# Attention's results stored by token, and the memory stage's first batch and weights loaded inside attention's last groups

## What is computed

```python
# 4 batches of 1024 tokens, 128 features, 16 heads of 8
q, k, v = heads(x @ w_attn.T + b_attn), ..., heads(x)
y_ar = softmax(causal(q @ k.T * scale)) @ v                 # attention
e    = v[1:] - y_ar[:-1]
qa, ka = -leaky_relu(-q[1:] * scale, 0.02), sigmoid(k2 * scale * 0.02)
y_ma = tril(qa @ ka.T) @ e                                  # memory, no softmax
out  = (y_ar + shift(y_ma)) @ w_proj.T + 2 * b_proj
```

## Time and profile before

| | us |
|---|---|
| median of 3 runs | 1926.33 |
| lowest and highest | 1923.79 to 1932.21 |
| profiled execution, its own time | 1940.25 |
| its span in the trace | 1938.2 |
| attention's last store issued | 626.4 |
| first DMA of memory | 628.6 |
| first DMA of ffn1 | 818.8 |
| PE busy share of the span | 72% |

### The profile page before, as it was taken

One profiled execution on the slowest core, in us unless ns is written; L12 is line 12 of the kernel. 1 busy time (PEld: TensorE's weight loads), 2 busy tenths in 40 slices (PEclk: granted clock), 3 DMA queues, 4 the chain that ended last, 5 costly groups with the idle time before them and its releaser, 6 DMA issues. The chain is left out here.

```text
span 1938.2 us, 29318 instructions
## 1 busy us (share of the span) xinstructions
PE 1394.9 (72%) x8975; PEld 721.5 (37%) x8976; DVE 1283.7 (66%) x2982; ACT 833.6 (43%) x1181; POOL 863.3 (45%) x761
## 2 busy tenths in 40 slices
PE   4459999999998488767598557586686545481992
PEld 1113333333332366644497222131131101351992
DVE  4567888888983144476233259999999998571333
ACT  3305666666666011122254267557466332120551
POOL 3401111121122333367366316876868665473662
PEclk9657999999999587878799778788797666796996
DMA  4721111111100765153232367785957763534335
GB/s 136 233 78 40 44 61 43 54 52 42 61 9 10 110 122 99 40 160 108 59 94 78 104 168 185 195 211 146 233 147 188 191 163 76 161 94 115 88 93 147
DMA packets 232076, 214.96 MB, mean 111 GB/s; under 512 B 66079, under 2 KB 201218, under 8 KB 229634
## 3 DMA queue, kind: packets, MB, share of 16 engines
q1 hardware_dynamic: 209934, 184.90, 37.6%
q0 software_dynamic: 9216, 19.02, 3.0%
q10 hardware_dynamic: 12800, 9.46, 1.6%
HBM read 149.46 MB, written 63.37 MB: 110 GB/s over the span
## 5 line engine op out<-in xcount | busy, mean ns | idle before, releaser
L772 ACT ACTIVATE attn_prob<-attn_ps_cols 128x1024 f32<-128x1024 f32 (+1 forms) x320 | 290.5, 940 | 231.1 <-PE attn_ps_cols L648 229.8
L2298 POOL TENSOR_TENSOR ssm_hc<-ssm_h,ssm_cb 128x1024 f32<-128x1024 f32 x128 | 301.4, 2356 | 169.8 <-DVE ssm_h L2281 122.3
L2281 DVE TENSOR_TENSOR_SCAN ssm_h<-ssm_decay,ssm_ps_u 128x1024 f32<-128x1024 f32 x128 | 292.6, 2286 | 17.2 <-DVE ssm_ps_u L2276 0.5
L798 POOL TENSOR_SCALAR_AFFINE_SELECT attn_prob<-attn_prob 128x512 f32<-128x512 f32 x128 | 81.2, 635 | 428.2 <-ACT attn_prob L772 428.2
L680 DVE CUSTOM_DVE_ANT_0 attn_ps_rows<-attn_ps_rows,const_mask_rows 128x384 f32<-128x384 f32 (+3 forms) x512 | 235.4, 521 | 42.6 <-PE attn_ps_rows L615 42.5
L615 PE MATMUL attn_ps_rows<-attn_ks,attn_qs 72*128 72x512 bf16 (+3 forms) x768 | 228.3, 351 | 42.3 <-DMA attn_qs<-parts_dram 29.1
L2232 PE MATMUL ssm_ps_u<-ssm_stack,ssm_spread 96*128 96x512 bf16 x256 | 100.3, 484 | 175.7 <-DVE ssm_h L2281 170.3
L2269 ACT ACTIVATE ssm_decay<-ssm_wide,ssm_aneg 128x1024 f32<-128x1024 f32 x128 | 146.0, 1146 | 179.0 <-DVE ssm_h L2281 120.6
L648 PE MATMUL attn_ps_cols<-attn_qs,attn_ks 75*128 75x512 bf16 (+3 forms) x768 | 194.4, 333 | 4.9 <-DMA attn_qs<-attn_nrows 4.1
L667 PE MATMUL attn_ps_o<-attn_prob,attn_vw 128*32 128x512 f32 (+3 forms) x1536 | 166.6, 506 | 0.3 <-POOL attn_prob L798 0.3
L685 DVE TENSOR_REDUCE attn_nm<-attn_ps_rows 128x1 f32<-128x512 f32 x256 | 157.7, 680 | 7.8 <-PE attn_ps_rows L615 7.8
(11 more groups left out here) (321 smaller groups left out, 2471.1 us busy)
## 6 DMA issues: line engine op xcount, KB each, us to landing
ssm_wide<-delta_dram SPq DMA_DIRECT2D x128, 512.0 KB, 6.4
attn_ks<-parts_dram SPq DMA_DIRECT2D x48, 192.0 KB
attn_qs<-parts_dram SPq DMA_DIRECT2D x48, 192.0 KB
parts_dram<-proj_parts SPq DMA_DIRECT2D x8, 768.0 KB, 3.8
ffn1e_x<-ex_dram SPq DMA_DIRECT2D x40, 130.0 KB, 2.3
ffn2e_x<-ex_dram SPq DMA_DIRECT2D x40, 130.0 KB, 2.2
split_dram<-ssm_parts SPq DMA_DIRECT2D x6, 768.0 KB, 4.4
ssm_stack<-split_dram SPq DMA_DIRECT2D x18, 256.0 KB, 4.3
```

The costliest lines, as they stand in the source:

```text
L772: nc.scalar.activation(prob[u % RING][:, heads[0]:heads[-1] + 1, 0:w], ps_cols[s % 2][:].rearrange("p b (x q) -> p (b x) q", x=len(heads) ...
L2281: nc.vector.tensor_tensor_scan(h[t % H_RING][:], decay[t % DECAY_RING][:], ps_u[t % 2][:], 0.0, ALU.mult, ALU.add).then_inc(scan_done, 1)
L2298: nc.gpsimd.tensor_tensor(hc[:, t % HC_RING, :], h[t % H_RING][:], cb[b % 2][:], ALU.mult).then_inc(hc_done, 1)
```

## The change

A class `Early` holds the tiles of even batches of the memory stage (rows, `kaT`, `qaT`, `yt`, `vs`, `x`, and the weights) and their semaphores. It is opened ahead of attention and given to both stages, so these tiles are there while attention runs. SP issues the loads of the weights and batch 0's rows after attention's group 12, and those of batch 0's `kaT`, `yt`, `vs`, `qaT` and `x` after group 13, behind a wait for the stores of batch 0's results. The memory stage's SP starts with batch 1. `yar` is laid out by token, 4096 by 128, and `yt` is one load a batch, in pieces of 128 numbers.

```diff
+class Early:
+    def load_rows(self, sp, dram):
+        feature = [dram["fT"][q].rearrange("(g d r) (b t) -> b r d g t", g=GPB, d=HD, b=B) for q in range(2)]
+        for r in range(RTILES):
+            sp.dma_start(self.kr[32 * r:32 * r + HD], feature[1][0, r]).then_inc(self.r_loaded, 16)
+            sp.dma_start(self.qr[32 * r:32 * r + HD], feature[0][0, r]).then_inc(self.r_loaded, 16)
+    def load_weights(self, sp, a):
+        sp.dma_start(self.wrow[:], a["w_proj"]).then_inc(self.w_loaded, 16)
+        sp.dma_start(self.brow[:], a["b_proj"].rearrange("(o n) -> o n", o=1).broadcast_to([P, P])).then_inc(self.w_loaded, 16)
+    def load_tokens(self, sp, dram, a):
+        sp.dma_start(self.kaT[:], dram["fT"][1, :, 0:T]).then_inc(self.ka_loaded, 16)
+        sp.dma_start(self.yt[:], dram["yar"][0:T, :].rearrange("(j p) d -> p j d", p=P)).then_inc(self.y_loaded, 16)
+        sp.dma_start(self.vs[:], dram["xn"][1:T + 1, :].rearrange("(j p) d -> p j d", p=P)).then_inc(self.v_loaded, 16)
+        sp.dma_start(self.qaT[:], dram["fT"][0, :, 0:T]).then_inc(self.qa_loaded, 16)
+        sp.dma_start(self.x[:], a["x"][0:T, :].rearrange("(j p) d -> p j d", p=P)).then_inc(self.x_loaded, 16)
...
 # attention
-        yar = dram["yar"].rearrange("g (c j p) n -> g c p j n", c=2, p=P)
+        yar = dram["yar"].rearrange("(b c j p) (g n) -> b g c p j n", b=B, c=2, p=P, g=GPB)
...
+                    if g == GROUPS - 4:
+                        early.load_weights(sp, a)
+                        early.load_rows(sp, dram)
+                    if g == GROUPS - 3:
+                        for ch in range(2):
+                            sp.wait_ge(y_stored[ch], GPB * 16)
+                        early.load_tokens(sp, dram, a)
...
 # memory
-            for g in range(GPB):
-                sp.dma_start(yt[k][:, :, g * GH * HD:(g + 1) * GH * HD], yar[i, g]).then_inc(y_loaded[k], 16)
+            sp.dma_start(yt[k][:], dram["yar"][i * T:(i + 1) * T, :].rearrange("(j p) d -> p j d", p=P)).then_inc(y_loaded[k], 16)
...
-                sp.dma_start(wrow[:], a["w_proj"]).then_inc(w_loaded, 16)
-                sp.dma_start(brow[:], a["b_proj"].rearrange("(o n) -> o n", o=1).broadcast_to([P, P])).then_inc(w_loaded, 16)
-                for i in range(B):
+                for i in range(1, B):
                     load_batch(sp, i)
```

More of the change, by code:

```diff
@@ L549, in bank_free, with __init__, attention @@
     return nth(g, same[-1] if same else -1)
-def attention(nc, dram, c):
+RTILES = 4
+class Early:
+    def __init__(self, nc, ctx):
+        self.m = m = Mem(nc, ctx, "early")
+        self.wrow, self.brow = m.sb("wrow", [P, P]), m.sb("brow", [P, P])
+        self.qr, self.kr = m.sb("qr", [P, GH, T]), m.sb("kr", [P, GH, T])
+        self.kaT, self.qaT = m.sb("kaT", [P, T]), m.sb("qaT", [P, T])
+        self.yt, self.vs, self.x = (m.sb(n, [P, BLK, D]) for n in ("yt", "vs", "x"))
+        self.w_loaded = m.sem("w_ld")
+        self.r_loaded, self.y_loaded, self.v_loaded, self.ka_loaded, self.qa_loaded, self.x_loaded = (
+            m.sem(n) for n in ("r_ld", "y_ld", "v_ld", "ka_ld", "qa_ld", "x_ld"))
+    def load_rows(self, sp, dram):
[12 more added lines that the diff above has]
+        sp.dma_start(self.x[:], a["x"][0:T, :].rearrange("(j p) d -> p j d", p=P)).then_inc(self.x_loaded, 16)
+def attention(nc, dram, c, early, a):
     with ExitStack() as ctx:
@@ L602, in store_y @@
             sp.sem_inc(passed, 1)
-            sp.dma_start(yar[at, ch], y[ch][:].rearrange("p j h d -> p j (h d)")).then_inc(y_stored[ch], 16)
+            sp.dma_start(yar[at // GPB, at % GPB, ch], y[ch][:].rearrange("p j h d -> p j (h d)")).then_inc(y_stored[ch], 16)
         def row_tile(k, n, loads, bank, free):
@@ L882 @@
 HALF = BLK // 2
-RTILES = 4
 AM_RING = 2
@@ L886, with memory @@
 HALVES = B * 2
-def memory(nc, dram, c, a):
+def memory(nc, dram, c, early, a):
     with ExitStack() as ctx:
         m = Mem(nc, ctx, "mem")
[L894 to L899, removed]
+        wrow, brow = early.wrow, early.brow
+        wT, bias2 = m.sb("wT", [P, P]), m.sb("bias2", [P, P])
+        qr, kr = [early.qr, m.sb("qr1", [P, GH, T])], [early.kr, m.sb("kr1", [P, GH, T])]
+        kaT, qaT = [early.kaT, m.sb("kaT1", [P, T])], [early.qaT, m.sb("qaT1", [P, T])]
+        yt, vs = [early.yt, m.sb("yt1", [P, BLK, D])], [early.vs, m.sb("vs1", [P, BLK, D])]
+        e = [m.sb(f"e{k}", [P, BLK, D]) for k in range(2)]
         ew = [m.sb(f"ew{k}", [P, BLK, HEADS, 32]) for k in range(2)]
         ka = [m.sb(f"ka{k}", [P, HALF, P]) for k in range(3)]
-        x, xb = ([m.sb(f"{n}{k}", [P, BLK, D]) for k in range(2)] for n in ("x", "xb"))
+        x = [early.x, m.sb("x1_in", [P, BLK, D])]
+        xb = [m.sb(f"xb{k}", [P, BLK, D]) for k in range(2)]
         x1 = [m.sb(f"x1{k}", [P, HALF, D]) for k in range(2)]
@@ L911, in memory @@
         ps_s = m.ps("ps_s", [P, UNIT])
-        w_loaded, w_turned, w_ready, bias_ready = (m.sem(n) for n in ("w_ld", "w_turned", "w_ready", "bias_ready"))
-        r_loaded, y_loaded, v_loaded, ka_loaded, qa_loaded, x_loaded = (m.pair(n) for n in ("r_ld", "y_ld", "v_ld", "ka_ld", "qa_ld", "x_ld"))
+        w_loaded = early.w_loaded
+        w_turned, w_ready, bias_ready = (m.sem(n) for n in ("w_turned", "w_ready", "bias_ready"))
+        r_loaded, y_loaded, v_loaded = [early.r_loaded, m.sem("r_ld")], [early.y_loaded, m.sem("y_ld")], [early.v_loaded, m.sem("v_ld")]
+        ka_loaded, qa_loaded, x_loaded = [early.ka_loaded, m.sem("ka_ld")], [early.qa_loaded, m.sem("qa_ld")], [early.x_loaded, m.sem("x_ld")]
         x1_stored = m.pair("x1_st")
@@ L921, in memory @@
         feature = [dram["fT"][q].rearrange("(g d r) (b t) -> b r d g t", g=GPB, d=HD, b=B) for q in range(2)]
-        yar = dram["yar"].rearrange("(b g) (j p) n -> b g p j n", b=B, p=P)
         def load_batch(sp, i):
@@ L966, in outputs @@
             if b == 0:
-                nc.tensor.wait_ge(y_loaded[k], (i // 2 + 1) * GPB * 16)
+                nc.tensor.wait_ge(y_loaded[k], (i // 2 + 1) * 16)
                 nc.tensor.wait_ge(qa_loaded[k], (i // 2 + 1) * 16)
@@ L1023, in make_e @@
             dve.wait_ge(v_loaded[k], n * 16 + 16)
-            dve.wait_ge(y_loaded[k], (n + 1) * GPB * 16)
+            dve.wait_ge(y_loaded[k], (n + 1) * 16)
             if i >= 2:
@@ L1182, in memory @@
         m.leave()
+        early.m.leave()
 EXPERTS, HIDDEN, TOP = 8, 256, 2
@@ L2618, in build @@
             "fT": scratch("fT_dram", (2, P, N)), "parts": scratch("parts_dram", (2 * PARTS, B, P, T), BF16),
-            "yar": scratch("yar_dram", (16, T, 32)), "x1": scratch("x1_dram", (N, D)),
+            "yar": scratch("yar_dram", (N, D)), "x1": scratch("x1_dram", (N, D)),
             "delta": scratch("delta_dram", (B, INNER, T)),
@@ L2628, in build @@
         project(nc, dram, c, {"x": rows, "w_attn": w_attn, "b_attn": b_attn, "w_k2": w_k2, "b_k2": b_k2})
-        attention(nc, dram, c)
-        memory(nc, dram, c, {"x": rows, "w_proj": w_proj, "b_proj": b_proj})
+        with ExitStack() as held:
+            early, rest = Early(nc, held), {"x": rows, "w_proj": w_proj, "b_proj": b_proj}
+            attention(nc, dram, c, early, rest)
+            memory(nc, dram, c, early, rest)
         ffn(nc, dram, c, experts, "ffn1", dram["x1"], None)
```

## The result

| | before | changed |
|---|---|---|
| median, us | 1929.27 (4 runs) | 1900.46 (4 runs) |
| lowest to highest | 1923.79 to 1936.92 | 1898.71 to 1908.86 |
| ratio | | 0.9842, 95% interval 0.9809 to 0.9875 |
| profiled execution | 1940.25 | 1898.71 |
| its memory stage | 190.2 | 158.1 |

The median fell by 28.8 us, against a forecast of 30.3. The forecast time, 1896.0 us, had been taken from the earlier median of 1926.33 (three runs); a fourth run moved that to 1929.27, and the measured 1900.46 is 4.5 us above the forecast and inside its range of 1874 to 1906. The length of the memory stage is taken here and in all experiments from POOL's first instruction of the stage to its first of ffn1. These two rows give it for the changed kernel, 781.90 - 623.76; before, they stand at 628.62 and 818.80.

What follows compares the result with a forecast made beforehand. PE was taken as the bound once it has its data, with loads costing late start, waits and clock. Savings 21.0 + 3.6 + 3.0 + 2.7 = 30.3 us off 1926.3 gave 1896.0 us, range 1874 to 1906.

Steps and rivals of the forecast that it cites:

- The sum: Whole kernel: the terms together save 30.3 us, for a median of 1896.0 us; chance 0.50.
- Attention, 0 us: Attention stage: 15 more DMAs issued beside it cost 0 us, at most 7 us.
- The start, 21.0 us: Memory stage's start: PE begins right behind the barrier, POOL ends last, outputs begin at 638.5 instead of 659.5, saving 21.0 us.
- Rest of batch 0 and batch 1, 3.6 us: Memory stage: batch 1's wait for `vs` goes (1.5 us on PE) and less low-clock work saves 2.1 us.
- The gap in batch 0: PE's 3.2 us gap in the middle of one product, likely an instruction fetch, was assumed to stay.
- Batches 2 and 3, 3.0 and 2.7 us: Memory stage: `vs` lands 26.1 us behind the first row DMA, so its waits shrink by 3.0 and 2.7 us.
- the sign: Batches 2 and 3: if `make_e` no longer waits for `vs`, rival 1 holds and the queue was misread.
- rival 1: Batches 2 and 3: small pieces filled the queue, waits for `vs` vanish, 51.2 us saved in all, 1875.1 us; chance 0.15.
- The reading of the queue: Batch loads: rows fill the queue, half of 16 engines busy at 53 GB/s, 1 MB taking some 20 us.
- Rival 2: Batch 0's products: PE's gap does not come back, saving 9.1 us more, 1886.9 us; chance 0.17.
- Rival 3: Batches 2 and 3: `vs` gains nothing behind the same rows and `kaT`; 24.6 us saved, 1901.7 us; chance 0.15.
- Rival 4: Memory stage: PE never reaches 2.4 GHz, the stage ends 15.5 us later, 1941.8 us; chance 0.03.

Runs made afterwards that it cites:

- e1: Changed kernel with the old token layout and four `yt` loads a batch put back, early loads kept: ratio 0.9826 to the kernel before, stage 158.2 us.
- e7: Changed kernel with SP instead of PE clearing attention's semaphores and POOL zeroing the second `ew` tile later: ratio 0.9849 to the kernel before, stage 152.3 us.
- e5: Changed kernel with SP held before batch 1's load until PE has done the products of blocks 0 to 2: stage 165.9 us.
- e2: Kernel before with only the token layout and single `yt` load added, no early loads: ratio 0.9998, stage 178.9 us.
- e3: Changed kernel without the row DMAs of batches 2 and 3, whose products use older rows: stage 137.1 us.

## Why the prediction was right, and where it was not

- **The sum.** 30.3 us were forecast, 28.8 measured in medians, 31.1 in the mean stage of two profiles each; direction, size and range held. In the first profiles the 32.0 us of the stage divide into 19.6 up to the outputs, 3.9 from there to batch 1's `make_e`, and 8.6 behind it, against 21.0, 3.6 and 5.7 in the forecast. The last term came out of another mechanism than the forecast's, and that it came near was luck.
- **Attention, 0 us:** right. The period and PE's work are unchanged though the load's DMA share rose to 0.44.
- **The start, 21.0 us:** 19.6 (30.9 less 11.3). The step "if PE begins by 632 ... what ends last is then POOL" failed by a little. PE began 4.0 us behind the barrier, and DVE's `e` came 1.25 us behind POOL's mask. e1 shows that early loads alone give the start, and e7 that PE's delay is its clearing of semaphores.
- **Rest of batch 0 and batch 1, 3.6 us:** 3.9, and the wait is gone. The gap in batch 0 came back, as assumed, with 3.3 us. The reason given, "it sits at one place of PE's instructions", was right as far as it went: the place is the same in every kernel and moves with PE's instruction count (e7). What it left out is the rows: in e5 the same instructions have no gap.
- **Batches 2 and 3, 3.0 and 2.7 us:** this step failed as a mechanism. The landing of `vs` was forecast at 26.1 us behind the rows and measured at 26.7 and 27.4. The wait I said would remain (5.6 and 3.1 us) did not, because PE stood 3.9 and 4.9 us ahead of it in new gaps, the first of them followed by work at 1.2 GHz, and DVE came later by that. PE stood 8.8 us in these two gaps, where before it had stood 8.8 and 6.0 us in waits: 6.1 us less, by chance near the 5.7 forecast. The other 2.5 us fit the shorter stretches at 1.2 GHz (12 and 8 us, against twice 14.4). By what I had named as the sign, rival 1 would have been shown; its 51 us did not come. e1 and e2 say why: the rows and not the pieces set the landing, and the single `yt`, while the rows drain, brings a gap behind record 825 that no kernel with four has.
- **The reading of the queue** was too simple. "Half of the 16 engines busy" while the rows drain holds from 710 on only; from 702 to 710 they were all busy before the change too (1.07 at 115 GB/s).
- **Rival 2** (the gap goes) fell in the changed kernel. Against it I had written that an instruction fetch "needs no data queue to be late"; if the gaps are fetches, e3 and e5 show the opposite. Its price of 9.1 us for a gap is about right: e3 lost two gaps and 21.1 us with them. **Rival 3** comes nearest to what one `yt` is worth: nothing that the runs can tell. **Rival 4** fell, the clock came back each time.
- **The profile's own spread** was missing from the argument: in this very stage the first profile before was 8 us longer than the second, and the first one after 6 us; in the difference the two nearly cancel.

## What to carry to other kernels

Load the next stage's first operands inside a stage that leaves the DMA queue idle: here 3.5 MB cost nothing and took 20 us off a barrier. Before giving one transfer fewer pieces or an earlier issue, look at what lies ahead of it in the queue, for the landing is set there. When a wait vanishes with less gain than it held, look for a gap on the bound engine with no releaser in the profile. Take a second profile before pricing anything below 8 us.

## What was not expected of the hardware

- PE had gaps of up to 7.4 us in the middle of its work, labelled "issue", always with row DMAs under way, and always at the same few places of its instruction stream, a multiple of about 126 matmuls apart. Taking 32 instructions out ahead of the stage moved the places by 15 or 16 matmuls. Without the rows (e3), or with them only 5 us old (e5), the same place had no gap. The length of a gap changes from execution to execution.
- With `yt` and `vs` queued behind the rows, all DMA engines showed busy at some 100 GB/s for 15 us; the same engines reached 337 GB/s at the end of a load. A DMA share near 1 is no sign of bandwidth used.
- 1 MB written to 32 partitions by DMAs of 8 took some 20 us; alternating partitions 0 and 64 took 2 to 3 us off.
- After the changed kernel's three gaps PE's clock came back 16, 12 and 8 us behind the restart, though PE was busy all that time.
